# LayerNorm's 1/sqrt moved to GpSimd, and work of the softmax half moved to other steps, in a four-layer hybrid block

## The chip, the core and the metric

The kernel runs on one core of one Trainium2 chip. The metric is the device time of one execution in microseconds, lower is better. The names of the engines are those of the profile: PE is TensorE (PEld its weight loads), DVE is VectorE, ACT is ScalarE, POOL is GpSimd, SP is SyncE, which here issues most of the DMAs.

## The reference

The input x has 8 sequences of 1024 tokens with 256 features. Four layers follow each other, each on the LayerNorm of the running x and each added to it:

```python
def _layernorm(x, axis=-1, eps=1e-05):
    m = jnp.mean(x, axis=axis, keepdims=True)
    v = jnp.var(x, axis=axis, keepdims=True)
    return (x - m) / jnp.sqrt(v + eps)

x = x + linear_attention(_layernorm(x))     # 16 heads of 16, q and k through softplus, causal
x = x + ffn(_layernorm(x))                  # gated scan
x = x + softmax_attention(_layernorm(x))    # 16 heads of 16, ALiBi bias, causal
x = x + ffn(_layernorm(x))

def step(c, xt):                            # the scan of ffn, over the 8 sequences
    ft = jax.nn.sigmoid(xt @ wf.T + c @ uf.T + bf)
    it = jax.nn.sigmoid(xt @ wi.T + c @ ui.T + bi)
    gt = jnp.tanh(xt @ wc.T + c @ uc.T + bc)
    return ft * c + it * gt, None
h = jnp.tanh(jnp.einsum('tbi,oi->tbo', x, wo) + c_final @ uo.T + bo)
```

## The kernel before, in words

**Two halves.** The first half (phase 1) is linear attention and the first ffn, the second (phase 2, the softmax half) is softmax attention and the second ffn. One sequence (1024 tokens, 8 tiles of 128) is a batch. Each half is a loop over stages b = -2 to 8, and each stage has 144 steps k = 0 to 143. In stage b the attention of batch b runs, and work of the neighbours is laid between its steps: LN1 (the LayerNorm ahead of the attention) of batch b+2, q, k and v of batch b+1, and of batch b-1 the output projection, LN2 (the LayerNorm ahead of the ffn) and the gates of the scan. Each engine has its own program, written out by hand in this order; a step is not a barrier, and engines wait for each other by semaphores alone.

**A step of the softmax half.** PE computes a block of turned scores for ACT's exp (L1092, two banks in turn) and, 48 steps ahead, a block of scores whose row maxima DVE takes (`max_unit`, L1443, two banks in turn). After each fourth step PE multiplies the exps by the values (L767). So a step needs PE, DVE and ACT, and none can be more than about two steps ahead. Between them PE gets "fill": pieces of the projections and gates, in steps 4 to 10 (q, k), 16 to 22 (output), 24 to 38 (v), 40 to 54 (q, k), 60 to 66 (x times Wo) and 68 to 137 (gates).

**What the change touches, by step of a softmax stage:**

- LN2 of batch b-1: DVE takes statistics (`bn_stats`, L1510) in steps 26 to 33, aggregates 8 tiles (`bn_aggr`, L1283) and gets 1/sqrt by 12 small dependent instructions, `newton` (L1286 to L1298), in steps 34 to 40; each waits for the one before through a semaphore. POOL then subtracts and multiplies (L1744) and makes the low bf16 part (L1765), and PE turns both parts at steps 56 and 58 (L545).
- LN1 of batch b+2: statistics in steps 62 to 69 (L1525), aggregation and `newton` in steps 70 to 76, then the same on POOL. PE turns the high part at step 0 and the low part at step 2 of the next stage; ACT and DVE each copy one bank of each part out of PSUM a step later (L1085, L1383).
- The gates: ACT writes tanhs (L1165), and for each of four groups DVE makes three operations of 128x512 in fp32 (L1270, L1272, L1275), in steps 91 to 93, 104 to 106, 127 to 129 and 140 to 142. At step 143 ACT rounds the new state to bf16 (L1025, one instruction of 2048 columns), and POOL subtracts to get the low part (L1680).
- POOL's queue, in order, in the part that matters: LN1's 8 + 4 instructions, `out_low` (L1699), `split_max` (L1735, L1739), four additions of a bias row to the residual (L1829). `split_max` at steps 95 and later feeds `turn_max`, a transpose that PE has at step 99 (L781) and waits for by the semaphore mx_parts; DVE's `combine` at step 95 (L1450) comes ahead of it.

In phase 1 the same `newton` runs on DVE in steps 34 to 40 and 70 to 76; LN2 is normalised by DVE itself there. Where batches begin or end (`by_vector`) DVE normalises too.

Of the kernel before, what the change touches and what calls it, by code (L numbers as in the profile page):

```python
# [5 lines left out]
F32 = mybir.dt.float32  # L6
BF16 = mybir.dt.bfloat16
I32 = mybir.dt.int32
# [4 lines left out]
P = 128  # L13
# [40 lines left out]
LEAD = GROUP + 12  # L54
HALF_ROWS = 64
# [77 lines left out]
def mixer_kernel(nc, x, weights, cols, rows, key_rows, masks, out):  # L133
    with ExitStack() as ctx:
# [22 lines left out]
        for phase in (1, 2):  # L157
            for name in ("xa_full", "stat1_", "stat2_", "ln_norm", "ln_low", "pk_raw", "v_ready", "o_taken", "o_low",
                         "x2_in", "x3_done", "x3_out"):
                sem[f"{name}{phase}"] = ctx.enter_context(nc.semaphore(f"{name}{phase}"))  # L160
# [37 lines left out]
        NY = sb("ln_newton", [P, NT], F32)  # L198
# [326 lines left out]
        def _(pe):  # L525
# [480 lines left out]
        def _(act):  # L1006
# [118 lines left out]
            def fill_softmax(b, k):  # L1125
                nb, pb, fb = b + 1, b - 1, b + 2
                if batch_in(nb):
                    if k in (1, 3):
                        turned_in(XT1, k // 2)
# [3 lines left out]
                if batch_in(nb) and k in (31, 39):  # L1133
                    values_in(nb, 2 * (31, 39).index(k))
                if batch_in(fb) and k in (5, 9, 33, 37) and (fb or k > 9):
                    tanh_h(fb, (5, 9, 33, 37).index(k))
                if batch_in(pb):
# [10 lines left out]
                    if k == BATCH - 1 and b < B:  # L1148
                        state_high()
# [93 lines left out]
        def _(dve):  # L1243
# [4 lines left out]

            def gates(phase, group):
# [13 lines left out]
            def gate_op(group, n):  # L1263
# [7 lines left out]
                elif n == 1:  # L1271
                    step(dve.scalar_tensor_tensor(out=TG[:, 1, :], in0=TG[:, 1, :], scalar=1.0, in1=TG[:, 2, :],  # L1272
                                                  op0=ALU.add, op1=ALU.mult))
                else:
                    dve.scalar_tensor_tensor(out=cs, in0=first, scalar=0.5, in1=TG[:, 1, :],  # L1275
                                             op0=ALU.mult, op1=ALU.add).then_inc(sem["gate_used"], 1)

            def newton(which, n):

                rs = RS[:, which, :]  # L1280
                if n == 0:
                    for t in range(NT):
                        i = dve.bn_aggr(MV[:, which, t, :], ST[:, t, :])  # L1283
                    step(i)
                elif n == 1:
                    step(dve.tensor_scalar(VE[:, :], MV[:, which, :, 1], LN_EPS, None, ALU.add))  # L1286
                elif n == 2:
                    step(dve.tensor_scalar(rs.bitcast(I32), VE[:, :].bitcast(I32), 1, None, ALU.logical_shift_right))
                elif n == 3:
                    step(dve.tensor_scalar(rs.bitcast(I32), rs.bitcast(I32), -1.0, float(0x5F3759DF),  # L1290
                                           ALU.mult, ALU.add))
                elif n % 3 == 1:
                    step(dve.tensor_tensor(NY[:, :], rs, rs, ALU.mult))
                elif n % 3 == 2:
                    step(dve.scalar_tensor_tensor(out=NY[:, :], in0=NY[:, :], scalar=-0.5, in1=VE[:, :],
                                                  op0=ALU.mult, op1=ALU.mult))
                else:
                    i = dve.scalar_tensor_tensor(out=rs, in0=NY[:, :], scalar=1.5, in1=rs, op0=ALU.add, op1=ALU.mult)  # L1298
                    step(i)

            NEWTON = 13
# [18 lines left out]
            for n in range(2):  # L1320
                dve.memset(V[n].rearrange("p n (h v) -> p (n h) v", v=HV)[:, :, HD:HD + 1], 1.0)
                dve.memset(OB[n][:, :], 0.0)
            dve.memset(QKP[1][0:3 * H, 0, :], 1.0)
# [160 lines left out]
            def take_banks(b, k):  # L1484
                nb, pb = b + 1, b - 1
                if batch_in(nb):
                    if k in (1, 3):
                        turned_in(XT1, k // 2)
# [397 lines left out]
```

## Time and profile before

| | us |
|---|---|
| Device time, median of 3 runs | 2546.62 (2545.64 to 2549.15) |
| Profiled execution, span from first to last instruction | 2551.4 |
| PE busy | 2128.6 (83%) |
| DVE busy | 1689.3 (66%) |
| ACT busy | 1264.4 (50%) |
| POOL busy | 782.0 (31%) |
| Mean granted clock of PE, share of full | 0.932 |

The profile gives one time for the profiled execution, its span; it is 4.8 us above the median of the timed runs. The chain of waits (the work that ended last, followed back from the last instruction) is 63% PE, 22% DVE, 7% ACT and 4% issue. The first half takes roughly 1090 us, the softmax half the rest, of which some 160 us per full stage.

### The profile page before, as it was taken

To read this page: it belongs to the slowest core of one execution; us is meant where nothing else is said; L and a number is where in the kernel's file an instruction comes from. 1 tells how busy PE (TensorE), PEld (TensorE's weight loads), DVE (VectorE), ACT (ScalarE), POOL (GpSimd) and SP (SyncE) were. 2 spreads that over 40 slices of the span, in tenths; PEclk is the share of its full clock that TensorE was granted. 3 is DMA by queue.
4 is the path that set the end of the run, shared out by engine and by line. 5 is a ranking of instruction groups with operands and counts; after the bars stand their busy time and mean duration, and the time that the engine had idled before them with its cause. 6 is when DMAs were issued, how large, how long until landed. Compare 5 with 4: busy or idle time off the path is not lost.

```text
span 2551.4 us, 58447 instructions
## 1 busy us (share of the span) xinstructions
PE 2128.6 (83%) x24737; PEld 1221.0 (48%) x24838; DVE 1689.3 (66%) x3766; ACT 1264.4 (50%) x2041; POOL 782.0 (31%) x658
## 2 busy tenths in 40 slices
PE   3558988888797886748889999999999999998963
PEld 1346565655565564424345444454444544444432
DVE  5546474656656454348878788788787888777327
ACT  2414334343424211213676667766677666766713
POOL 2132323414143011144424335243362432412110
PEclk8789989999999988877999999999999999999977
DMA  3201010101011011134414233142331322213063
GB/s 97 66 18 43 26 51 18 62 24 51 18 35 35 18 51 47 37 110 113 117 44 121 72 84 118 41 120 76 85 117 35 117 59 76 76 35 124 12 231 132
DMA packets 131541, 179.28 MB, mean 70 GB/s; under 512 B 9121, under 2 KB 95137, under 8 KB 131281
## 3 DMA queue, kind: packets, MB, share of 16 engines
q1 hardware_dynamic: 129104, 175.02, 22.6%
q8 instruction: 196, 3.21, 0.5%
q10 hardware_dynamic: 2176, 0.52, 0.1%
q14 instruction: 65, 0.52, 0.1%
HBM read 97.40 MB, written 77.59 MB: 69 GB/s over the span
## 4 chain that ended last, share of the span: by engine, by line
PE 63%; DVE 22%; ACT 7%; issue 4%; POOL 2%; DMA 1%; SPq 0%; DVEq 0%; POOLq 0%; ACTq 0%
PE general L893 11%; PE general L579 10%; PE out_of_heads L767 9%; DVE maxima L1443 8%; PE scores L722 6%; PE general L565 4%; PE general L904 4%; PE general L545 3%; PE turned_scores L736 3%; PE out_of_heads L653 3%; PE out_of_heads L663 2%; PE scores L611 2%; PE general L553 2%; PE out_of_heads L787 1%; PE scores L671 1%
## 5 line engine op out<-in xcount | busy, mean ns | idle before, releaser
L1443 DVE TENSOR_REDUCE maxima<-scores 128x1 f32<-128x512 f32 (+3 forms) x1536 | 795.3, 552 | 228.9 <-PE scores L698 117.8
L1092 ACT ACTIVATE probs_turned<-turned_scores 128x512 f32<-128x512 f32 x1152 | 679.6, 601 | 354.7 <-PE turned_scores L698 181.4
L722 PE MATMUL scores<-k_stacks,q_stacks 59*128 59x512 bf16 (+3 forms) x1536 | 444.4, 335 | 59.2 <-DVE maxima L1443 51.6
L736 PE MATMUL turned_scores<-q_stacks,k_stacks 61*128 61x512 bf16 (+3 forms) x1536 | 436.1, 329 | 9.4 <-ACT probs_turned L1092 9.4
L722 PEld LDWEIGHTS scores<-k_stacks,q_stacks 59*128 59x128 bf16 x1536 | 124.1, 94 | 285.8 <-DVE maxima L1443 218.1
L1765 POOL TENSOR_TENSOR ln_low<-ln 128x512 bf16<-128x512 f32 x128 | 138.4, 1088 | 286.6 <-DVE ln L1425 262.6
L1744 POOL TENSOR_SCALAR ln<-x_for_attention,ln_mean_var,ln_rstd 128x256 f32<-128x256 f32 x104 | 127.9, 1239 | 187.9 <-DVEq L1532 96.6
L1680 POOL TENSOR_TENSOR state_low<-state_doubled,state_high 128x2048 bf16<-128x2048 f32 x14 | 57.0, 4068 | 363.0 <-ACT state_high L1025 363.0
L1019 ACT ACTIVATE gate_tanhs<-general,feature_vectors 128x512 f32<-128x512 f32 x96 | 66.0, 687 | 204.4 <-PE general L579 200.2
L1408 DVE TENSOR_SCALAR reciprocals<-scores 128x16 f32<-128x16 f32 x64 | 11.1, 173 | 224.4 <-PE scores L671 224.3
L767 PE MATMUL out_of_heads<-probs_turned,values 128*17 128x512 f32 (+3 forms) x1536 | 154.6, 498 | 0.0
L767 PE MATMUL out_of_heads<-probs_turned,values_odd_and_heads_out 128*17 128x512 f32 (+3 forms) x1536 | 153.0, 494 | 1.3 <-ACT probs_turned L1092 1.3
L1060 ACT COPY values_odd_and_heads_out<-out_of_heads 128x512 f32<-128x512 f32 x64 | 37.4, 585 | 233.6 <-PE out_of_heads L663 231.9
L736 PEld LDWEIGHTS turned_scores<-q_stacks,k_stacks 61*128 61x128 bf16 x1536 | 125.5, 94 | 52.0 <-ACT probs_turned L1092 18.6
L893 PE MATMUL general<-ln_turned_high,w_high 64*128 64x512 bf16 (+1 forms) x596 | 123.2, 379 | 26.7 <-ACT values L1154 11.4
L698 PE MATMUL scores<-mask_scores,identity_halves_swapped 64*128 64x128 bf16 (+1 forms) x640 | 133.9, 209 | 0.0
L698 PE MATMUL scores<-mask_scores,identity 64*128 64x128 bf16 (+1 forms) x640 | 133.8, 209 | 0.0
L698 PE MATMUL turned_scores<-mask_turned,identity 64*128 64x128 bf16 (+1 forms) x640 | 131.9, 206 | 0.0
L698 PE MATMUL turned_scores<-mask_turned,identity_halves_swapped 64*128 64x128 bf16 (+1 forms) x640 | 131.8, 206 | 0.0
L893 PE MATMUL general<-ln_turned_low,w_high 64*128 64x512 bf16 (+1 forms) x599 | 124.2, 378 | 0.1
L893 PE MATMUL general<-ln_turned_high,w_low 64*128 64x512 bf16 (+1 forms) x600 | 123.4, 377 | 0.0
L565 PE MATMUL general<-w_high,ln_turned_high 128*128 128x256 bf16 x384 | 107.0, 279 | 16.2 <-DVE ln_turned_low L1383 10.0
(252 smaller groups left out, 5347.8 us busy)
## 6 DMA issues: line engine op xcount, KB each, us to landing
x_after_attention<-x_residual SPq DMA_DIRECT2D x16, 1024.0 KB, 5.3
x_times_wo<-x_wo_out SPq DMA_DIRECT2D x64, 256.0 KB, 2.1
q_stacks<-q_stack SPq DMA_DIRECT2D x64, 256.0 KB, 4.7
k_stacks<-k_stack SPq DMA_DIRECT2D x64, 256.0 KB, 4.9
x_for_attention<-in_x SPq DMA_DIRECT2D x8, 1024.0 KB, 5.5
x_residual<-in_x SPq DMA_DIRECT2D x8, 1024.0 KB, 5.4
x_for_attention<-x_after_attention SPq DMA_DIRECT2D x8, 1024.0 KB, 5.5
ffn_h<-x_times_wo SPq DMA_DIRECT2D x32, 256.0 KB, 6.1
```

The source lines that it names most:

```text
L565: mm = pe.matmul(bank[:, n * D:(n + 1) * D], src[xp][:, k, at], W[wp][:, m, k, :], start=(i == 0), stop=(i == len(todo) - 1))
L579: mm = pe.matmul(bank[:, :], W[wp][:, m, k, e * P:(e + 1) * P], src[xp][:, k, c * CH:(c + 1) * CH], start=(n == 0), stop=(n == len(todo) - 1))
L698: return pe.matmul(columns[:, first:last + 1:step, :], eye, m, start=False, stop=(n == 1))
L722: mx = pe.matmul(bank_s[:, first * P:(first + tiles) * P], QS[at_s:at_s + QROWS, r, i * P:(i + 1) * P], KS[at_s:at_s + QROWS, r, k0 * P:(k ...
L736: ex = pe.matmul(bank_t[:, first * P:(first + tiles) * P], KS[at_t:at_t + KROWS, r, j * P:(j + 1) * P], QS[at_t:at_t + KROWS, r, i0 * P:(i ...
L767: mm = pe.matmul(OB[half][32 * g:32 * g + HV, at:at + tiles * P], values[:, j, HV * h:HV * (h + 1)], PR[:, (HEADS * unit + g) % SLOTS, fir ...
L893: return pe.matmul(bank[:, :], W[wp][rows_, m, k, e * P:(e + 1) * P], src[xp][rows_, k, c * CH:(c + 1) * CH], start=start, stop=stop)
L904: return pe.matmul(bank[:, tile * D:(tile + 1) * D], src[xp][rows_, k, t0:t0 + P], W[wp][rows_, m, k, :], start=start, stop=stop)
L1092: nc.scalar.activation(PR[:, s % SLOTS, :], TB[s % 2][:, :], ACT.Exp).then_inc(sem["ex_taken"], 1)
L1443: r = dve.tensor_reduce(MP[:, gg % 2, g, at:at + 1], max_bank[m][:, first * P:(first + tiles) * P], AX.X, ALU.max)
L1744: i = pool.tensor_scalar(XN[:, t, :], src[:, t, :], MV[:, which, t, 0:1], RS[:, which, t:t + 1], ALU.subtract, ALU.mult)
L1765: pool.tensor_tensor(pair(XL, c), pair(XN, c), top(pair(XN, c)), ALU.subtract).then_inc(sem[f"ln_low{phase}"], 1)
```

## The change

The table of steps is now at the head of the file, and the step of each operation is looked up in it. In words:

- `newton` is gone from DVE. DVE's `aggregate` does the 8 `bn_aggr` and signals POOL; `layer_norm` on POOL adds eps and raises to the power -0.5 (two instructions on 128x8), and then signals rstd. Where DVE normalises, it waits for that signal. This holds in both halves.
- Softmax half: LN2's statistics are in steps 25 to 37 with the aggregation at 38; LN1's are spread over steps 63 to 82 with the aggregation at 83.
- A group's three gate operations are 4 steps apart and not in neighbouring steps; the last one of the last group is in step 5 of the next stage. Stage 8, which has no attention, keeps them together.
- ACT's rounding of the state is in two halves of 1024 columns, at steps 19 and 23 of the next stage, and POOL's `state_low` follows after `sum_h`.
- PE turns the high part of LN1 at step 140, for batch b+2, and the low part at step 0.
- POOL's wait for the constants' DMAs is no longer at its start but ahead of the first write to the buffer that those DMAs read.

```diff
+LN2_AT = (25, 26, 27, 29, 33, 34, 35, 37)
+LN1_AT = (63, 66, 69, 71, 74, 75, 78, 82)
+GATE_AT = (((91, 95, 99), (103, 107, 111), (127, 131, 135), (139, 143)),
+           ((91, 92, 93), (104, 105, 106), (127, 128, 129), (140, 141, 142)))
+GATE_REST = 5
+HIGH_AT = (19, 23)
+TURN_AT = (140, 0)
...
             def turns(b, k):
-                if batch_in(b + 1) and k in (0, 2):
-                    if k == 0:
-                        pe.wait_ge(sem["ln_low2"], 4 * norms_to(2, "ln1", b + 1))
-                    turn_both(XN, XL, k // 2)
+                if batch_in(b + 2) and k == TURN_AT[0]:
+                    pe.wait_ge(sem["ln_norm2"], 4 * norms_to(2, "ln1", b + 2))
+                    turn_both(XN, XL, 0)
+                if batch_in(b + 1) and k == TURN_AT[1]:
+                    pe.wait_ge(sem["ln_low2"], 4 * norms_to(2, "ln1", b + 1))
+                    turn_both(XN, XL, 1)
...
-                    if k == BATCH - 1 and b < B:
-                        state_high()
+                if batch_in(pb - 1) and k in HIGH_AT:
+                    half = HIGH_AT.index(k)
+                    if half == 0:
+                        act.wait_ge(sem["gate_used"], w.next("gate_used"))
+                    i = nc.scalar.copy(CP[0][:, half, :], CS[:, half, :])
+                    if half:
+                        i.then_inc(sem["state_high"], 1)
...
+            def aggregate(phase, which, taken):
 
-            NEWTON = 13
+                dve.wait_ge(sem["dve_step"], w.at(taken))
+                for t in range(NT):
+                    i = dve.bn_aggr(MV[:, which, t, :], ST[:, t, :])
+                i.then_inc(sem[f"stat{which + 1}_{phase}"], 1)
...
+                    for group, places in enumerate(GATE_AT[b == B]):
+                        if k in places:
+                            gate_op(group, places.index(k))
+                if batch_in(pb - 1) and k == GATE_REST:
+                    gate_op(3, 2)
...
             pool.wait_ge(sem["const_ready"], w.next("const_ready"))
-            pool.wait_ge(sem["const_stored"], w.next("const_stored", 128))
...
             def layer_norm(phase, which, src, b):
                 done = 4 * (norms_to(phase, f"ln{which}", b) - 1)
+                pool.wait_ge(sem[f"stat{which}_{phase}"], b + 1)
+                pool.tensor_scalar(VE[:, :], MV[:, which - 1, :, 1], LN_EPS, None, ALU.add
+                                   ).then_inc(sem["pool_step"], 1)
+                pool.wait_ge(sem["pool_step"], w.next("pool_step"))
+                pool.tensor_tensor(RS[:, which - 1, :], VE[:, :], minus_half[:, :], ALU.pow
+                                   ).then_inc(sem[f"rstd{which}_{phase}"], 1)
...
-                if batch_in(pb - 1):
-                    state_low(2, pb - 1)
                 if batch_in(pb):
                     out_low(pb, 1)
...
+                if batch_in(pb - 1):
+                    state_low(2, pb - 1)
+                if batch_in(fb):
                     for c in (2, 3):
                         add_h(fb, c)
```

**DVE, steps 34 to 40 of a softmax stage (end of LN2).** Each line of `maxima` is one or more steps of `max_unit`. Before:

```order
L1283 BN_AGGR ln_mean_var<-ln_stats 128x2 x8
L1286 TENSOR_SCALAR ln_var_eps<-ln_mean_var 128x8
L1443 TENSOR_REDUCE maxima<-scores 128x1 x2
L1288 TENSOR_SCALAR ln_rstd<-ln_var_eps 128x8
L1290 TENSOR_SCALAR ln_rstd<-ln_rstd 128x8
L1443 TENSOR_REDUCE maxima<-scores 128x1 x2
L1293 TENSOR_TENSOR ln_newton<-ln_rstd 128x8
L1295 SCALAR_TENSOR_TENSOR ln_newton<-ln_newton,ln_var_eps 128x8
L1443 TENSOR_REDUCE maxima<-scores 128x1 x2
L1298 SCALAR_TENSOR_TENSOR ln_rstd<-ln_newton,ln_rstd 128x8
```

The same engine at the same place in the changed kernel:

```order
L1516 BN_STATS ln_stats<-x_residual 128x6
L1446 TENSOR_REDUCE maxima<-scores 128x1 x2
L1516 BN_STATS ln_stats<-x_residual 128x6
L1446 TENSOR_REDUCE maxima<-scores 128x1 x4
L1516 BN_STATS ln_stats<-x_residual 128x6
L1446 TENSOR_REDUCE maxima<-scores 128x1 x2
L1302 BN_AGGR ln_mean_var<-ln_stats 128x2 x8
L1470 COPY values_odd_and_heads_out<-general 128x32x16
```

The small dependent instructions between the maxima are gone; the last statistics and the aggregation stand where they were.

**ACT, from the last gate tanh of a stage to the first steps of the next.** Before, with the rounding of the state between the exps and both copies of LN1's turned parts after it:

```order
L1165 ACTIVATE gate_tanhs<-general,feature_vectors 128x512
L1092 ACTIVATE probs_turned<-turned_scores 128x512 x4
L1025 CAST state_high<-state_doubled 128x2048
L1092 ACTIVATE probs_turned<-turned_scores 128x512 x2
L1085 COPY ln_turned_high<-general 128x1024
L1092 ACTIVATE probs_turned<-turned_scores 128x512 x2
L1085 COPY ln_turned_low<-general 128x1024
```

And in the changed kernel:

```order
L1181 ACTIVATE gate_tanhs<-general,feature_vectors 128x512
L1101 ACTIVATE probs_turned<-turned_scores 128x512 x2
L1094 COPY ln_turned_high<-general 128x1024
L1101 ACTIVATE probs_turned<-turned_scores 128x512 x4
L1094 COPY ln_turned_low<-general 128x1024
L1101 ACTIVATE probs_turned<-turned_scores 128x512 x4
```

The high part's copy has moved to step 141, the low part's to step 1, and the rounding is gone from here.

**POOL, from LN1 to the bias additions.** Before, from the last third of LN1, which DVE signalled at the end of step 76:

```order
L1744 TENSOR_SCALAR ln<-x_for_attention,ln_mean_var,ln_rstd 128x256 x2
L1765 TENSOR_TENSOR ln_low<-ln 128x512 x2
L1699 TENSOR_TENSOR attention_out_low<-attention_out 128x8x128
L1735 CAST maxima_parts<-maxima 128x16 x2
L1739 TENSOR_TENSOR maxima_parts<-maxima,maxima_parts 128x16 x2
L1829 TENSOR_TENSOR x_residual<-x_residual,row_vectors 128x512 x4
```

In the changed kernel the queue is the same behind LN1, which now begins with two more instructions and is signalled at the end of step 83:

```order
L1759 TENSOR_SCALAR ln_var_eps<-ln_mean_var 128x8
L1762 TENSOR_TENSOR ln_rstd<-ln_var_eps,minus_half 128x8
L1752 TENSOR_SCALAR ln<-x_for_attention,ln_mean_var,ln_rstd 128x256 x4
L1779 TENSOR_TENSOR ln_low<-ln 128x512
L1752 TENSOR_SCALAR ln<-x_for_attention,ln_mean_var,ln_rstd 128x256 x2
L1779 TENSOR_TENSOR ln_low<-ln 128x512
L1752 TENSOR_SCALAR ln<-x_for_attention,ln_mean_var,ln_rstd 128x256 x2
L1779 TENSOR_TENSOR ln_low<-ln 128x512 x2
L1705 TENSOR_TENSOR attention_out_low<-attention_out 128x8x128
L1743 CAST maxima_parts<-maxima 128x16 x2
```

`split_max` (the last row) still stands behind LN1 and `out_low`.

## Rows read from the trace of the kernel before

**Rows 1.** Windows, two whole stages: busy time of each engine, its instructions, granted clock.

```profile
1474.86:1634.01 159.15, 153.00 (x1895) 77.64 (x1894) 128.90 (x293) 111.10 (x194) 65.32 (x63) 1.00 0.31 88
1794.72:1955.42 160.70, 154.54 (x1895) 78.49 (x1894) 128.98 (x293) 111.31 (x194) 65.31 (x63) 0.99 0.31 87
```

**Rows 2.** Windows around LN2 and LN1 of stage 4, columns PE, PEld, DVE, ACT, POOL.

```profile
1827.00:1848.00 21.00, 18.85 (x269) 9.97 (x267) 20.05 (x62) 13.39 (x25) 6.27 (x9) 1.00 0.45 124
1876.00:1887.00 11.00, 10.79 (x155) 6.08 (x150) 10.31 (x44) 6.66 (x13) 0.93 (x1) 1.00 0.61 175
```

**Rows 3.** Chain of waits, LN2 of stage 4: start, duration, what.

```profile
1831.84 0.69 DVE maxima L1443
...
1839.58 0.18 DVE ln_var_eps L1286
...
1841.62 0.87 DVE ln_newton L1293
...
1847.31 0.23 PE scores L722
```

**Rows 4.** Chain of waits, the first LayerNorm of the softmax half.

```profile
1093.82 0.65 DVE ln_mean_var L1283 x8
1094.50 0.18 DVE ln_var_eps L1286
...
1097.03 4.85 DVE ln L1425 x8
```

**Rows 5.** Chain of waits, LN2 of one stage of phase 1.

```profile
578.53 0.18 DVE ln_newton L1293
...
580.73 0.18 DVE ln_rstd L1298
```

**Rows 6.** Chain of waits, the edge between stages 4 and 5.

```profile
1955.42 1.76 issue
...
1959.21 1.89 PE general L545 x16
```

**Rows 7.** Window just after that edge.

```profile
1959.00:1962.40 3.40, 3.19 (x28) 2.22 (x32) 1.91 (x6) 2.64 (x5) 2.42 (x1) 0.50 0.28 55
```

**Rows 8.** Timeline of POOL in stage 3, from LN1 to the bias additions.

```profile
1725.36 4.83 POOL L1744 TENSOR_SCALAR ln<-x_for_attention,ln_mean_var,ln_rstd 128x256 f32<-128x256 f32 x4 [16.37 <-DVEq L1532]
...
1738.98 1.89 POOL L1699 TENSOR_TENSOR attention_out_low<-attention_out 128x1024 bf16<-128x1024 f32 x1
1745.42 0.33 POOL L1735 CAST maxima_parts<-maxima 128x16 bf16<-128x16 f32 x2 [4.55 <-DVE maxima L1450]
...
1746.18 4.95 POOL L1829 TENSOR_TENSOR x_residual<-x_residual,row_vectors 128x512 f32<-128x512 f32 x4
```

**Rows 9.** Timeline of DVE there: steps 82 and 83, and two gate operations.

```profile
1730.42 1.47 DVE L1443 TENSOR_REDUCE maxima<-scores 128x1 f32<-128x512 f32 x2
...
1739.70 1.72 DVE L1270 SCALAR_TENSOR_TENSOR gate_tanhs<-gate_tanhs,state_doubled 128x512 f32<-128x512 f32 x1
...
1741.94 0.67 DVE L1272 SCALAR_TENSOR_TENSOR gate_tanhs<-gate_tanhs 128x512 f32<-128x512 f32 x1
```

**Rows 10.** Timeline of PE there, `turn_max` at step 99.

```profile
1749.24 0.24 PE L781 MATMUL scores<-identity,maxima_parts 128*64 128x128 bf16 x1
```

**Rows 11.** Timeline of DVE in stage 0, steps 82 and 83.

```profile
1262.19 1.28 DVE L1443 TENSOR_REDUCE maxima<-scores 128x1 f32<-128x512 f32 x2
```

**Rows 12.** Timeline of PE in stage 0, `turn_max` at step 99.

```profile
1278.55 0.24 PE L781 MATMUL scores<-identity,maxima_parts 128*64 128x128 bf16 x1
```

**Rows 13.** Groups by line, POOL: a small cast, and its costliest elementwise form.

```profile
L1715 POOL TENSOR_SCALAR probs_turned<-qk_block,mask_even_odd 128x1024 f32<-128x1024 f32 x16 | 46.3, 2903 | 33.7 <-DVE qk_block L1421 33.7
...
L1735 POOL CAST maxima_parts<-maxima 128x16 bf16<-128x16 f32 x64 | 10.5, 196 | 357.6 <-DVE maxima L1450 357.6
```

**Rows 14.** Chain of waits, stage 7: LN2 on POOL, and the rounding of the state.

```profile
2320.91 4.83 POOL ln L1744 x4
...
2422.35 1.60 issue
```

More of the change, by code:

```diff
@@ L1271, in gate_op @@
                 elif n == 1:
-                    step(dve.scalar_tensor_tensor(out=TG[:, 1, :], in0=TG[:, 1, :], scalar=1.0, in1=TG[:, 2, :],
-                                                  op0=ALU.add, op1=ALU.mult))
+                    dve.scalar_tensor_tensor(out=TG[:, 1, :], in0=TG[:, 1, :], scalar=1.0, in1=TG[:, 2, :],
+                                             op0=ALU.add, op1=ALU.mult).then_inc(sem["dve_step"], 1)
+                    taken["gate"] = w.later("dve_step")
                 else:
+                    dve.wait_ge(sem["dve_step"], w.at(taken["gate"]))
                     dve.scalar_tensor_tensor(out=cs, in0=first, scalar=0.5, in1=TG[:, 1, :],
                                              op0=ALU.mult, op1=ALU.add).then_inc(sem["gate_used"], 1)
[L1278 to L1299, printed above, removed]
-            NEWTON = 13
+            def aggregate(phase, which, taken):
[3 more added lines that the diff above has]
+                i.then_inc(sem[f"stat{which + 1}_{phase}"], 1)
             def last_state_low(phase, half):
@@ L1564, in fill @@
                         if k == 33:
-                            step(i)
-                    if 34 <= k < 41:
-                        for n in range(2 * (k - 34), min(2 * (k - 34) + 2, NEWTON)):
-                            newton(1, n)
+                            i.then_inc(sem["dve_step"], 1)
+                            taken[1] = w.later("dve_step")
+                    if k == 34:
+                        aggregate(1, 1, taken[1])
                     if k in (45, 47, 48, 50):
                         if k == 45:
+                            dve.wait_ge(sem["rstd2_1"], pb + 1)
                             dve.wait_ge(sem["xt_dve"], turned_before(1, "ln2", pb))
@@ L1583, in fill @@
                         if at == 69:
[L1584 to L1589 removed]
+                            i.then_inc(sem["dve_step"], 1)
+                            taken[0] = w.later("dve_step")
+                    if at == 70:
+                        aggregate(1, 0, taken[0])
                     if by_vector(1, 1, fb) and at == 77:
+                        dve.wait_ge(sem["rstd1_1"], fb + 1)
                         if turned_before(1, "ln1", fb):
@@ L1711, in split_q @@
                 pool.wait_ge(sem["phi_done"], 4 * nb + 2 * e + 1)
+                if nb == 1 and e == 0:
+                    pool.wait_ge(sem["const_stored"], w.next("const_stored", 128))
                 if nb >= 2:
```

77 lines of the change are left out of this document (37 added, 40 removed).

## The prediction

> **What bounds the kernel now.** I read the busy shares first: PE is near its limit and DVE has a third of its time free, so most work taken from DVE should be worth nothing. The windows of whole stages say the same of the softmax half: in a stage of 159 or 161 us PE is busy for 153 to 155 us and DVE for 129 us [rows 1]. So what counts is where a stage is not PE's. Two windows answer that. Around LN2 (steps 25 to 43) DVE is busy for 20.05 of 21.00 us and PE for only 18.85; around LN1 (steps 67 to 78) DVE has 10.31 of 11.00 us, but PE has 10.79, so both are full there [rows 2]. The chain of waits, read last, confirms it: from 1831.84 to 1847.31 us, 15.5 us without a break, every piece is DVE's, maxima with statistics and `newton` instructions between them, and then it goes back to PE [rows 3]. At the edge of two stages the chain is ACT's: 1.76 us of "issue" behind the start of the state's rounding, then exps and the copy of the turned LN1, until PE's second turning begins at 1959.21, 3.8 us after 1955.42 [rows 6]. Right behind it PE's granted clock is 0.50, which is 1.2 GHz, for 3.4 us [rows 7]. The stage that began without such a fall took 159.15 us and the one with it 160.70, with the same 1895 matmuls [rows 1]: the fall costs 1.5 us. Four edges of the same kind show such a fall.
>
> **LN2 in the softmax half.** One `newton` costs, from the end of the aggregation to the first normalisation with nothing between, 1097.03 - 1094.50 = 2.5 us: 12 instructions of 0.18 us and their waits [rows 4]. In a stage its pieces stand between maxima at nearly the same price; one of them even takes 0.87 us [rows 3]. The aggregation (0.65 us) stays. In the 15.5 us of DVE's own chain 2.5 us go. PE is not idle beneath: it has 2.15 us free in the 21 us window [rows 2], and its modelled ends stretch where it waits, so the gain can be as low as 1.0; above, with the locked 0.87 us instruction and the earlier statistics, it is 2.8. I take 2.5, because the chain is DVE's throughout. Six stages (1 to 6): 15.0 us. In stage 7, which has no q, k, v of a next batch, PE is not late; there the chain goes on through POOL's LN2 from 2320.91 [rows 14]. The signal now comes two steps earlier and without `newton`: 2.5 + 2 x 0.76 (a step of maxima) - 0.6 (new work on POOL, below) = 3.4 us.
>
> **LN1 in the softmax half.** The same 2.5 us go from DVE, but PE is full there [rows 2]; at the end of that stretch some PE time was lost. I take 0.3 us for six stages, 1.8 us (between 0 and 1.9 each).
>
> **The new instructions on POOL.** No row of before shows a power on POOL. The nearest is a small one, 0.20 us for a cast of 16 columns; the costliest elementwise instruction takes 2.9 us, though for 1024 columns [rows 13]. The new ones have 8 columns, so I take the small row: 0.2 for eps, 0.3 for the power, 0.15 for two semaphores, 0.65 us in all; I keep 0.4 and 3 as ends.
>
> **Serial LayerNorms.** Five times DVE makes a LayerNorm with nothing beside it: two at the start, the last of phase 1, the first of phase 2 [rows 4] and the last of all. Each gives 2.5 - 0.65 = 1.9 us: 9.5 us. The turning of the first of phase 2 no longer waits for the first low part: 1.1 us more. Sum 10.6 us. POOL's wait for the constants, moved away from its start, must go with it, since POOL's signal now stands ahead of the first normalisation.
>
> **LN2 in phase 1.** The chain of one stage holds two pieces of `newton`, three instructions from 578.53 and two up to 580.91 [rows 5], 1.0 us together; seven stages show the same: 7.0 us (3 to 9). There DVE normalises from step 45 on, ten steps after the signal, so POOL's 0.65 us is hidden. LN1 in phase 1 is on no chain: nothing.
>
> **The edge.** The rounding leaves ACT's queue between the exps (1.76 us of the chain), and one of two turnings leaves the first three steps, with its copy, for step 140, where PE has no fill, but where DVE is busy with gate operations; DVE gets the 0.69 us copy there and gives two of its gate operations away. Of the 3.8 us [rows 6] the two exps stay, and some of the turning's 1 us comes back at step 140. I take 2.0 us, with 1.0 and 3.2 as bounds, for the six edges from 1-2 to 6-7: 12.0 us. The four falls of the clock go with the idle time that comes ahead of them, 4 x 1.5 = 6.0 us. At the last edge the rounding's 1.6 us goes [rows 14]. Sum 19.6 us. In its new place the rounding lies in steps 19 and 23, each half about 1 us, where PE's fill is long and ACT has slack; I charge 1.0 us for all stages. `state_low` (4 us) moves with it on POOL, ahead of add_h, which waits for a tanh of step 33 anyway: nothing.
>
> **What gets worse: POOL at step 99.** LN1 is now signalled at the end of step 83 and not 76. Before, POOL began LN1 at 1725.36, was through with it and with `out_low` at 1740.87, and then sat idle for 4.55 us until `combine` let `split_max` go [rows 8]. This idle time is used up. In before, from the end of step 83 on DVE (1730.42 + 1.47 = 1731.89) [rows 9] to `turn_max` on PE (1749.24) [rows 10] there are 17.35 us. In the changed kernel these must hold: 0.3 for the statistics of step 82, 0.65 aggregation, 0.65 the new instructions, 13.62 LN1 (1725.36 to 1738.98), 1.89 `out_low`, 0.76 `split_max` [rows 8], and 0.6 for two gate operations that now meet LN1. That is 18.5 us. So PE's `turn_max` waits for POOL, DVE and ACT run out two steps behind it, and the stage loses 1.1 us at this place, in stages 1 to 5: -5.5 us. In stage 0, which has no gates and little fill, only 1278.55 - 1263.47 = 15.1 us are there [rows 11, 12] against 17.9: -2.8 us. Stages 6 and 7 have no LN1, and spreading the gate operations gives 0.8 us in each, since the first took 1.72 us against 0.67 for its neighbour [rows 9]: +1.6. Sum -6.7 us (-20 to 0).
>
> The gate operation of 1.72 us began at 1739.70, while POOL's `out_low` ran until 1740.87; it ended 0.55 us after that, so it waited for POOL's instruction to end [rows 8, 9]. The Trainium skill (SBUF — State Buffer, Who interferes with whom) has this as a rule: a DVE instruction with two SBUF inputs and a GpSimd instruction that reads SBUF exclude each other for a whole instruction, and the first to start wins. The trace agrees here. By the rule all of the operations at steps 91, 95, 99 and 103 would meet a POOL that has no gap, each waiting up to 1.2 us or holding POOL for 0.67 us, and the stage would lose about 1 us more than I charge, 5 us in all; the forecast would then be 2502 us, inside its own range.
>
> **Sum.** 15.0 + 3.4 + 1.8 + 10.6 + 7.0 + 19.6 - 1.0 - 6.7 = 49.7 us. The profiled execution's own time, its span, is 2551.4 us, so 2501.7; it is 4.8 us above the median of the timed runs, 2546.62, and I take the same distance off: 2497 us, 2.0% faster.
>
> **Rivals.**
>
> 1. PE is the bound everywhere. For it: PE's busy time in a stage leaves only 6 us [rows 1]. Against it: the chain around LN2 has no PE in it [rows 3]. Then LN2 gives 1.0 and not 2.5, an edge 1.0 and not 2.0: 9 + 6 = 15 us less, 2512 us.
> 2. The power is slow on POOL, about 2 us. It counts wherever POOL is waited for: at step 99 of six stages and in five serial LayerNorms, 11 x 1.7 = 19 us: 2516 us. Nothing in the trace speaks for or against it but the small instructions [rows 13].
> 3. The stall moves instead of going: PE's wait at step 99 takes the clock down as the one at the edge did [rows 7], six times 1.5 us, and the four falls at the edges stay: 9 + 6 us, 2512 us. For it: the wait would be as long as PE's pause at an edge. Against it: each wait at step 99 is a single one.
> 4. Slower than before: the same queue of POOL at step 99 decides. It needs 50 us in all, that is a power of more than 0.3 + 50/11 = 4.8 us on POOL in these 11 places; at 6.3 us, twice the costliest instruction of [rows 13], it would be 2497 + 66 = 2563 us.
>
> **How the numbers follow.** Forecast 0.57 (2485 to 2508), rival 1 0.16, rival 2 0.13, rival 3 0.10, rival 4 0.04. All but the last and the far end of the second (0.02) are faster by over 0.2%, about what a measurement can tell from no change here: faster 0.94, within it 0.02, slower 0.04. The range goes from 2478 (an edge at 3.2, LN2 at 2.8 and nothing lost at step 99 would be 2481) to 2522, past rivals 1 to 3.
>
> **What would show it.** Right: the chain around LN2 has no small DVE instructions and changes to PE early; a full stage of the softmax half takes about 155 us; no 0.50 clock at the edges; PE's L781 of step 99 waits for POOL's `maxima_parts` for 1 to 2 us in stages 0 to 5, and POOL has no idle time between LN1, `out_low` and `split_max`; the power takes 0.2 to 0.4 us. Wrong: a power of microseconds; a chain that goes through POOL in the middle of the stage for several us; stages 1 to 5 no shorter than 158 us; a new wait at step 140, where PE's turning needs ACT's last gate tanh, or at steps 19 and 23, where exps wait behind the rounding.

## The result, and the profile after

| | before | changed |
|---|---|---|
| Device time, median of 4 runs, us | 2547.89 (2545.64 to 2551.01) | 2531.91 (2528.0 to 2538.07) |
| Ratio, 95% interval | | 0.9933 (0.9914 to 0.9952) |
| Span of the profiled execution, us | 2551.4 | 2536.3 |
| DVE busy, us | 1689.3 | 1644.2 |
| POOL busy, us | 782.0 | 852.0 |

The change makes the kernel 0.7% faster, not the 2.0% of the forecast, and 2531.91 us lies 10 us outside the range. The sign was right and the size was missed by 35 us. The profiled execution is the longest of the four, 6 us above their median. Sections 1 and 4 of the profile's page show what shifted: DVE's share of the chain fell from 22% to 16%, and POOL's rose from 2% to 7%.

```profile
PE 2113.1 (83%) x24737; PEld 1221.7 (48%) x24838; DVE 1644.2 (65%) x3383; ACT 1260.8 (50%) x2048; POOL 852.0 (34%) x722
...
PE 65%; DVE 16%; ACT 8%; POOL 7%; issue 4%; DMA 1%; SPq 0%; DVEq 0%; POOLq 0%; ACTq 0%
```

Two whole stages of the changed kernel, stages 1 and 3, beside the stages 2 and 4 of [rows 1] (columns PE, PEld, DVE, ACT, POOL, granted clock, DMA share, GB/s). They are hardly shorter than the 159.15 and 160.70 us of before, with DVE's busy time unchanged to 1 us although `newton` has left it, and PE's lower by up to 2.8 us. 3 us of what DVE is busy with is a blocked instruction, as shown below.

```profile
1314.49:1473.13 158.64, 151.77 (x1896) 78.61 (x1894) 127.99 (x268) 108.96 (x193) 66.91 (x66) 0.99 0.31 88
1633.06:1791.92 158.86, 151.77 (x1896) 78.71 (x1894) 128.38 (x269) 110.57 (x195) 70.91 (x67) 0.99 0.31 88
```

**Where in a stage.** ACT's exp (L1092 before, L1101 after) starts once a step, 1152 times in all. The difference in the time between two such starts, after less before, places every microsecond. Each figure is that of the profiled executions, in us:

| steps | stage 0 | each of stages 1 to 5 | stage 6 | stage 7 | all stages |
|---|---|---|---|---|---|
| 24 to 47 (LN2) | 0.0 | -2.97 | -2.18 | -2.88 | -19.9 |
| 48 to 59 | 0.0 | 0.05 to 0.27 | 0.05 | 2.30 | 2.9 |
| 60 to 95 (LN1) | -3.8 | -1.04 | 0.0 | 0.0 | -9.1 |
| 96 to 119 (step 99) | 8.0 | 5.35 to 6.65 | 0.0 | 0.3 | 38.2 |
| 120 to 143 and 0 to 23 (edge) | 0.6 | -1.9, with a fall of the clock gone -3.5 | -2.5 | -1.8 | -17.8 |

The sum is -5.7 us. Another -8.2 us stand ahead of the first exp (phase 1 and the serial LayerNorms) and -1.3 us behind the last: -15.1 us before rounding, the difference of the two spans. So everywhere but at one step 53 us were won, where the forecast had 49.7 + 8.3 = 58 us without its charge for step 99, and 38 us of them went at that step.

**LN2.** The chain of waits of the changed kernel in stage 4, at the place of [rows 3]. DVE's own piece (its end is shown) has no small `newton` instruction in it any more, and from 1824.86 us the chain is PE's. Where DVE's chain had 15.5 us without a break, its longest piece is now 6.0 us, from 1818.88 to 1824.86.

```profile
1822.96 0.34 DVE ln_stats L1516
1823.29 0.59 DVE maxima L1446
1823.88 0.33 DVE ln_stats L1516
1824.22 0.60 DVE maxima L1446
1824.86 0.39 PE scores L729
1825.32 0.44 PE general L911 x8
```

**Step 99.** The chain of waits in stage 3. From the end of the aggregation to PE's turning of the parts it is POOL's for 19.9 us.

```profile
1724.04 0.56 DVE ln_mean_var L1302 x8
...
1724.68 0.25 POOL ln_var_eps L1759
...
1725.01 1.68 POOL ln_rstd L1762
...
1726.78 4.83 POOL ln L1752 x4
...
1741.42 1.85 POOL attention_out_low L1705
1743.27 0.75 POOL maxima_parts L1743 x2
...
1744.09 0.40 POOL maxima_parts L1747 x2
...
1744.54 0.31 PE scores L788
```

The timeline of POOL there, answering to [rows 8]. The power takes 1.67 us where 0.3 was assumed. Of the eight instructions of LN1 (L1752), the first four take 4.83 us as before, and the two later pairs 2.86 and 2.95 us. A pair with nothing beside it takes 2.42 us (a row of the first experiment's kernel further down).

```profile
1725.01 1.67 POOL L1762 TENSOR_TENSOR ln_rstd<-ln_var_eps,minus_half 128x8 f32<-128x8 f32 x1
...
1732.61 2.86 POOL L1752 TENSOR_SCALAR ln<-x_for_attention,ln_mean_var,ln_rstd 128x256 f32<-128x256 f32 x2
...
1736.47 2.95 POOL L1752 TENSOR_SCALAR ln<-x_for_attention,ln_mean_var,ln_rstd 128x256 f32<-128x256 f32 x2
1739.39 2.03 POOL L1779 TENSOR_TENSOR ln_low<-ln 128x512 bf16<-128x512 f32 x2
1741.38 1.89 POOL L1705 TENSOR_TENSOR attention_out_low<-attention_out 128x1024 bf16<-128x1024 f32 x1
1743.22 0.79 POOL L1743 CAST maxima_parts<-maxima 128x16 bf16<-128x16 f32 x2
```

DVE and PE on the same timeline. The gate operation of step 99 takes 3.54 us and not 0.68: it begins while POOL runs `ln_low`, and ends 0.6 us after `out_low` does. PE stands still for 3.92 us ahead of L788, and a matmul of 512 columns then takes 0.60 us where it took 0.38.

```profile
1740.28 3.54 DVE L1295 SCALAR_TENSOR_TENSOR state_doubled<-gate_tanhs 128x512 f32<-128x512 f32 x1
```

```profile
1739.26 0.38 PE L729 MATMUL scores<-k_stacks,q_stacks 59*128 59x512 bf16 x1
...
1744.54 0.31 PE L788 MATMUL scores<-identity,maxima_parts 128*64 128x128 bf16 x1 [3.92 <-POOL maxima_parts L1747]
1744.78 0.60 PE L729 MATMUL scores<-k_stacks,q_stacks 59*128 59x512 bf16 x1
```

Windows show the clock there (columns as above). PE has 0.02 us of work in 3.60 us, and in the 3.40 us behind it the granted clock is 0.50, that is 1.2 and not 2.4 GHz.

```profile
1740.60:1744.20 3.60, 0.02 (x3) 0.00 (x0) 3.22 (x1) 0.00 (x0) 3.52 (x5) 1.00 0.94 299
1744.20:1747.60 3.40, 3.06 (x23) 1.31 (x25) 0.94 (x2) 1.07 (x3) 3.40 (x5) 0.50 0.47 149
```

In the softmax steps before, 20.5 us ran at half clock, 13.7 of them right behind four edges; in the changed kernel it is 44.4 us, of which 34 us stand behind step 99 in stages 0 to 5. None stands right behind an edge, but the fall that before had in step 1 of stage 7 is not gone: it stands in step 10 and costs about 1.6 us there.

### The profile page after: what moved, and what is told of

Read it like the earlier page. It is cut to its first block, busy times and chain, and to the rows that moved or that the text cites. A ratio compares the mean times of both kernels' runs of the same rounds, so it can differ in the third digit from the quotient of the medians.

```text
span 2536.3 us, 58000 instructions
## 1 busy us (share of the span) xinstructions
PE 2113.1 (83%) x24737; PEld 1221.7 (48%) x24838; DVE 1644.2 (65%) x3383; ACT 1260.8 (50%) x2048; POOL 852.0 (34%) x722
## 4 chain that ended last, share of the span: by engine, by line
PE 65%; DVE 16%; ACT 8%; POOL 7%; issue 4%; DMA 1%; SPq 0%; DVEq 0%; POOLq 0%; ACTq 0%
PE general L900 11%; PE general L586 10%; PE out_of_heads L774 9%; PE scores L729 6%; PE general L911 4%; DVE maxima L1446 4%; PE general L572 4%; PE turned_scores L743 3%; POOL ln L1752 3%; PE general L552 3%; PE out_of_heads L660 3%; PE scores L618 2%; PE out_of_heads L670 2%; PE general L560 2%; PE scores L705 1%
## 5 line engine op out<-in xcount | busy, mean ns | idle before, releaser
L1101 ACT ACTIVATE probs_turned<-turned_scores 128x512 f32<-128x512 f32 x1152 | 678.7, 601 | 333.0 <-PE turned_scores L705 174.7
L729 PE MATMUL scores<-k_stacks,q_stacks 59*128 59x512 bf16 (+3 forms) x1536 | 447.3, 337 | 49.7 <-DVE maxima L1446 46.2
L1069 ACT COPY values_odd_and_heads_out<-out_of_heads 128x512 f32<-128x512 f32 x64 | 37.4, 585 | 222.3 <-PE out_of_heads L670 220.6
L1759 POOL TENSOR_SCALAR ln_var_eps<-ln_mean_var 128x8 f32<-128x8 f32 x32 | 7.9, 248 | 389.4 <-DVE ln_mean_var L1302 389.4
L1752 POOL TENSOR_SCALAR ln<-x_for_attention,ln_mean_var,ln_rstd 128x256 f32<-128x256 f32 x104 | 132.4, 1283 | 1.4
L1393 DVE TENSOR_TENSOR probs_turned<-scores,mask_keep 128x512 f32<-128x512 f32 x128 | 84.1, 685 | 67.7 <-PE turned_scores L618 67.5
L1743 POOL CAST maxima_parts<-maxima 128x16 bf16<-128x16 f32 x64 | 16.0, 280 | 324.4 <-DVE maxima L1453 324.4
```

What stands on the lines that cost most here:

```text
L729: mx = pe.matmul(bank_s[:, first * P:(first + tiles) * P], QS[at_s:at_s + QROWS, r, i * P:(i + 1) * P], KS[at_s:at_s + QROWS, r, k0 * P:(k ...
L1101: nc.scalar.activation(PR[:, s % SLOTS, :], TB[s % 2][:, :], ACT.Exp).then_inc(sem["ex_taken"], 1)
L1752: i = pool.tensor_scalar(XN[:, t, :], src[:, t, :], MV[:, which, t, 0:1], RS[:, which, t:t + 1], ALU.subtract, ALU.mult)
```

## The experiments

Times are medians of 4 runs with 95% intervals against the kernel before on the same chip. "Gap" is PE's idle time ahead of L788 at step 99, "loss" the difference to before in steps 96 to 107, both for stages 1 to 5. The medians of the kernel before in these comparisons lie between 2547.89 and 2549.8 us, so times of different rows can be compared to within about 2 us.

| | us | ratio | gap | loss |
|---|---|---|---|---|
| changed kernel | 2531.91 | 0.9933 (0.9914 to 0.9952) | 3.92 | 5.4 to 6.7 |
| e1 LN1's statistics early | 2489.7 | 0.9768 (0.9753 to 0.9782) | none | 0 |
| e2 split_max inside LN1 | 2496.89 | 0.9792 (0.9778 to 0.9807) | none | 0.6 |
| e3 product for power | 2502.99 | 0.982 (0.9804 to 0.9837) | 1.63 | 1.95 |
| e4 power twice (one run) | 2538.09 | | 4.90 | 6.8 to 7.1 |
| e5 only the power moved | 2509.57 | 0.9843 (0.9829 to 0.9858) | none | 0 |
| e6 = e1, rounding back | 2512.33 | 0.9853 (0.9837 to 0.987) | none | 0 |
| e7 = e1, turning back | 2489.43 | 0.9764 (0.9749 to 0.9778) | none | 0 |
| e8 first gate group together | 2518.71 | 0.9879 (0.9864 to 0.9894) | 2.59 | 2.9 to 4.1 |
| e9 power and rounding only | 2488.15 | 0.9759 (0.9743 to 0.9776) | none | 0 |

**e1: LN1's statistics back in steps 62 to 69.** The theory is that POOL's queue at step 99 costs what is missing.

```diff
-LN1_AT = (63, 66, 69, 71, 74, 75, 78, 82)
+LN1_AT = (62, 63, 64, 65, 66, 67, 68, 69)
```

> The changed kernel with LN1's statistics back in steps 62 to 69 and its aggregation in step 70; all else as changed. Theory A (the loss is the wait of PE at step 99 for split_max, which stands behind LN1 in GpSimd's queue, because LN1 is signalled at step 83): in the changed kernel steps 96 to 107 are 5.4 to 6.7 us longer in stages 1 to 5 and 8.0 us in stage 0; all of that goes, and up to 1 us per stage comes back around LN1 on VectorE: 2532 - 30 - 8 + 7 = about 2501 us, PE's gap ahead of L788 zero, no half clock in mid-stage. Rival B (VectorE and GpSimd meet at the shared port because the gate operations are spread, whatever LN1 does): steps 96 to 107 keep 3 us or more each, 2515 to 2532 us.

It took 2489.7 us, 42 less than the changed kernel, by this one line. No gap and no half clock are left in the softmax steps. In the traces 37.9 of the 45.7 us between the two kernels lie in steps 96 to 119. The timeline of POOL in stage 3: LN1's last pair takes 2.42 us, `out_low` ends at 1707.05, and POOL then has 7.21 us to spare before `combine` lets `split_max` go, more than the 4.55 us of before.

```profile
1700.77 2.42 POOL L1752 TENSOR_SCALAR ln<-x_for_attention,ln_mean_var,ln_rstd 128x256 f32<-128x256 f32 x2
...
1705.15 1.90 POOL L1705 TENSOR_TENSOR attention_out_low<-attention_out 128x1024 bf16<-128x1024 f32 x1
1714.26 0.72 POOL L1743 CAST maxima_parts<-maxima 128x16 bf16<-128x16 f32 x2 [7.21 <-DVE maxima L1453]
```

**e2: split_max ahead of the last quarter of LN1.** The signal stays late, and only the order on POOL changes.

```diff
+                    if inside and c == 2:
+                        inside()
...
-                    layer_norm(2, 1, XA, fb)
+                    layer_norm(2, 1, XA, fb, (lambda: split_max(GROUPS * b + 3)) if early else None)
```

> The changed kernel with one thing moved in GpSimd's queue: in stages 0 to 5 split_max of step 95 stands inside LN1, behind its third quarter, ahead of the last pieces and of out_low; LN1 is signalled at step 83 as in the changed kernel. Theory A: the wait at step 99 goes although LN1 is as late as before, 2532 - 30 - 7 = about 2496 us; GpSimd may now wait for VectorE's combine for up to 1 us, which costs nothing. Rival B (port): gate operations still meet LN1 and out_low, and with VectorE blocked for up to 3.5 us at step 99 its maxima come late: PE loses 2 us or more per stage, 2508 to 2520 us.

The gaps are gone here too, at 2496.89 us. In stage 3 the CAST of `split_max` now starts 6 us before `out_low` and not behind it. So it is the place of `split_max` in POOL's queue that PE waits for, and LN1 itself, late as it is, costs only 0.6 us a stage.

```profile
1714.14 0.72 POOL L1743 CAST maxima_parts<-maxima 128x16 bf16<-128x16 f32 x2
...
1720.16 1.89 POOL L1705 TENSOR_TENSOR attention_out_low<-attention_out 128x1024 bf16<-128x1024 f32 x1
```

**e3: the power replaced by a product**, so the 1/sqrt is left out of the output, and nothing else is.

```diff
-                pool.tensor_tensor(RS[:, which - 1, :], VE[:, :], minus_half[:, :], ALU.pow
+                pool.tensor_tensor(RS[:, which - 1, :], VE[:, :], minus_half[:, :], ALU.mult
```

> The changed kernel with GpSimd's power replaced by a product of the same shape, so that the output lacks the 1/sqrt; everything else, waits included, is as changed. It prices the power, 1.67 us in the profile of the changed kernel, against about 0.2 us. Theory A: 1.45 us less in each of six waits at step 99 (8.7 us, more where the clock then does not fall), in five LayerNorms with nothing beside them (7 us) and in stage 7 (1.5 us): about 2514 us, the gap ahead of L788 2.4 us instead of 3.9. Rival C (the power is hidden, and the gap is made by the locked instructions): under 3 us in all, 2529 us or more.

The product takes 0.20 us, 1.47 less than the power, so the small row that I had taken [rows 13] holds for a product and not for a power. The gap shrinks by 2.3 us and not by 1.47 alone, since LN1 also takes 13.65 us and not 14.60: the gate operations meet POOL's queue elsewhere (the one at step 99 takes only 1.25 us). No fall of the clock follows the gap in stages 1 to 5. The time falls by 28.9 us to 2502.99. By the count of 11 places it would be 16 us: the power's price is nearly doubled by what it sets off.

```profile
1710.51 0.20 POOL L1762 TENSOR_TENSOR ln_rstd<-ln_var_eps,minus_half 128x8 f32<-128x8 f32 x1
```

```profile
1727.61 0.24 PE L788 MATMUL scores<-identity,maxima_parts 128*64 128x128 bf16 x1 [1.63 <-POOL maxima_parts L1747]
```

**e4: a second power on POOL**, whose result nobody reads, in the LN1 of the softmax half.

```diff
+                if phase == 2 and which == 1:
+                    pool.tensor_tensor(spare[:, :], VE[:, :], minus_half[:, :], ALU.pow)
```

> The changed kernel with a second, unused power ahead of the first, in LN1 of the softmax half alone. Theory A: every us that GpSimd is later is a us of PE at step 99: the gap ahead of L788 grows from 3.9 to 5.6 us in stages 1 to 5, the whole by 6 x 1.7 = 10 us, about 2542 us. Rival C: the gap stays at 3.9 to 4.5 us.

The gap is 4.90 us, 1.0 more, and not the full 1.67 us. POOL's queue shows why: it is shifted, so the gate operations fall elsewhere in it; LN1 takes 14.30 us and `split_max` 0.76, against 14.60 and 1.22, and the pair of L1753 shown below is back at 2.43 us. One run gave 2538.09 us, the same as the profiled execution of the changed kernel (2538.07), so the price of the longer gap isn't shown by the total; the loss in steps 96 to 107 is 6.8 to 7.1 us against 5.4 to 6.7.

```profile
1728.08 1.67 POOL spare_power L1764
1729.74 1.62 POOL ln_rstd L1765
...
1737.56 2.43 POOL ln L1753 x2
```

**e5: the kernel before with nothing but 1/sqrt on POOL**, the aggregation signalling at steps 34 and 70; every other part of the change is left out but the move of the wait for the constants, which the power needs.

> The kernel before, with only 1/sqrt moved to POOL in both halves; statistics, gate operations, rounding and turning stand where they were, and the aggregation now signals at step 70 (LN1) and step 34 (LN2), six steps earlier than newton's end did. Theory (DVE's chain around LN2 is what the power relieves, and step 99 is lost only where LN1 is signalled late): LN2 gives 2.5 to 2.9 us in each of stages 1 to 6, stage 7 gives 3, phase 1 and the serial LayerNorms together 8 to 10, step 99 has no gap ahead of the turn and steps 96 to 107 are within 0.5 us of before, the edges give nothing: 2549 - (16 + 3 + 9) = 2521 us, 2515 to 2527. Rival (the gain at steps 36 to 47 comes from the statistics' new steps): that range changes by under 1 us a stage, and the time is about 2535. Rival (two more POOL instructions are enough for a gap at step 99, whatever the signal): a gap over 1 us there, 2530 or more.

2509.57 us, 11 less than I expected and 22 less than the whole change. Steps 36 to 47 gain 2.82 us a stage with the statistics where they were, so that gain is the power's. Steps 72 to 95 gain 1.17 us in stages 1 to 5 and 3.0 us in stage 0. The edge between two stages gains nothing, but two of the four falls of the clock there are gone (1.5 us each). A full stage of it, windows:

```profile
1769.51:1924.67 155.16, 151.40 (x1892) 78.36 (x1892) 123.99 (x268) 110.77 (x194) 69.25 (x68) 1.00 0.31 90
```

**e6: e1 with the rounding of the state whole at step 143 again**, and the last gate group at 140 to 142.

```diff
-                if batch_in(pb - 1) and k in HIGH_AT:
-                    ...
+                if batch_in(pb) and k == BATCH - 1 and b < B:
+                    state_high()
```

> LN1's statistics in steps 62 to 69 as in e1_ln1_early, and the state's rounding whole at step 143 again, with the last group of gate operations at 140 to 142. Theory (of the edge's gain the larger part is ACT's rounding, the 1.76 us of issue in before's chain): six edges lose 1.3 to 1.8 us each against e1_ln1_early, 2498 to 2500 us. Rival (the turning of LN1 is what counts at the edge): under 4 us lost, 2492 to 2494. Rival (the clock's fall comes back with the idle time too): half clock stretches reappear right behind the edges, and the loss is above 12 us.

It lost 22.6 us against e1, as much as the last of the three cases wanted, though only a fifth of it is the clock's: 2.18 us in steps 132 to 143 of each stage, 1.62 in the last, and 4.5 us in steps 0 to 11, where four falls of the clock are back (13.7 us at half clock against none). The chain of waits at the edge between stages 3 and 4 shows the 1.63 us behind it, as [rows 6] did:

```profile
1771.22 0.17 ACT state_high L1034
1771.39 1.63 issue
1773.03 1.07 ACT probs_turned L1101 x2
```

**e7: e1 with both turnings of LN1 at steps 0 and 2 again.**

```diff
-                if batch_in(b + 2) and k == TURN_AT[0]:
-                    ...
+                if batch_in(b + 1) and k in (0, 2):
+                    ...
```

> LN1's statistics in steps 62 to 69 as in e1_ln1_early, and both turnings of LN1 at steps 0 and 2 again. Theory (the rounding is the larger part of the edge): the turning costs 0.5 to 1.2 us an edge, 2493 to 2497 us, in steps 0 to 11, with steps 132 to 143 giving a little of it back. Rival (the turning counts most): 8 us or more lost, 2498 or above.

2489.43 us, the same as e1. Steps 132 to 143 get 0.60 us a stage back, and steps 0 to 11 lose 0.24. Moving the turning had no worth; I had expected 0.5 to 1.2 us an edge.

**e8: the changed kernel with the first gate group back in steps 91 to 93.**

```diff
-GATE_AT = (((91, 95, 99), (103, 107, 111), (127, 131, 135), (139, 143)),
+GATE_AT = (((91, 92, 93), (103, 107, 111), (127, 131, 135), (139, 143)),
```

> The changed kernel with the first group of gate operations back at steps 91, 92 and 93, so that none stands at step 99, where DVE's gate operation waited 3.54 us for POOL. Theory (the gap at step 99 is POOL's queue of LN1, out_low and split_max; the blocked DVE operation lies beside it): the gap stays at 3 to 4 us, stages 1 to 5 change by under 1 us each, 2528 to 2532 us. Rival (the spread gate operations and the shared SBUF port make the gap): the gap falls below 2 us and the time to 2515 or less.

I had expected no more than 1 us a stage. The gap fell by 1.33 us to 2.59, the loss by 2 to 3.7 us, and the time by 13 us to 2518.71. So the blocked gate operation isn't beside the path: when it ends its wait it holds POOL's CAST (0.79 us for two in the changed kernel, 0.33 here), and LN1 takes 14.07 us (1720.97 to 1735.04) and not 14.60. These two are 1.0 of the 1.33 us; the other 0.33 us is that PE comes to step 99 that much later, since steps 84 to 95 give 0.33 us less. In stage 0 the gap stays at 5.30 us. In four of stages 1 to 5 no fall of the clock follows the shorter gap; the stage with a fall lost 4.08 us, those without 2.91. So one fall costs 1.2 us at this place. The rest of the gap stays, so both theories have a part. POOL's timeline:

```profile
1735.04 1.89 POOL L1705 TENSOR_TENSOR attention_out_low<-attention_out 128x1024 bf16<-128x1024 f32 x1
1736.88 0.33 POOL L1743 CAST maxima_parts<-maxima 128x16 bf16<-128x16 f32 x2
```

```profile
1737.73 0.24 PE L788 MATMUL scores<-identity,maxima_parts 128*64 128x128 bf16 x1 [2.60 <-POOL maxima_parts L1747]
```

**e9: two parts alone, the power on POOL and the rounding at steps 19 and 23.** Statistics, gate operations and turning stand as before.

```diff
-LN2_AT = (25, 26, 27, 29, 33, 34, 35, 37)
+LN2_AT = (26, 27, 28, 29, 30, 31, 32, 33)
-GATE_AT = (((91, 95, 99), (103, 107, 111), (127, 131, 135), (139, 143)),
+GATE_AT = (((91, 92, 93), (104, 105, 106), (127, 128, 129), (140, 141, 142)),
...
-                if batch_in(pb - 1) and k == GATE_REST:
-                    gate_op(3, 2)
```

(against e7's kernel)

> Only two parts of the change: 1/sqrt on POOL, and ACT's rounding of the state at steps 19 and 23; statistics, gate operations and turning stand as in the kernel before. Theory (these two make the whole gain, the spread statistics and gate operations are worth nothing): against e5_power_alone six edges gain 2.3 us and the last one 1.6, and what clock falls are left at edges go, so 2488 to 2493 us, the same as e7_turning_back (2489.43) within 0.2%. Rival (part of the edge's gain is the last group's third gate operation, which left step 142): steps 132 to 143 gain under 1.5 us an edge and the time is 2495 or more. Rival (spreading LN2's statistics helps): steps 24 to 47 lose over 0.5 us a stage against e7_turning_back, 3 us or more in all.

2488.15 us, 2.4% under before and 1.7% under the changed kernel. It has the lowest median, and e1 and e7 are the same within their spread. Against e7, steps 24 to 47 differ by 0.01 us a stage: spreading LN2's statistics brings 0.43 us in steps 24 to 35 and costs 0.43 in 36 to 47. All of the changed kernel's gain is in these two parts, and the other moves bring nothing or cost. A stage of it:

```profile
1759.80:1912.64 152.84, 150.73 (x1896) 78.36 (x1894) 123.25 (x269) 110.54 (x194) 69.13 (x67) 1.00 0.32 91
```

## Why the prediction was wrong, step by step

- **What bounds the kernel: right.** DVE around LN2, ACT's rounding at the edge, PE elsewhere. Rival 1 is out: LN2 and the edge gave their full size.
- **LN2 in the softmax half: right.** 15.0 us forecast for stages 1 to 6; 17.0 measured (five times 2.97 and 2.18), and e5 shows that it is `newton`'s. In stage 7 the 3.4 us came to 0.6, since 2.30 of 2.88 us went again in steps 48 to 59, behind POOL's LN2; a fall of the clock stands there in the changed kernel, and e7, without one, loses 0.96.
- **LN1: sized too low.** 1.8 us forecast, 9.1 measured in steps 60 to 95, of which 3.8 in stage 0. I had read "PE is full" from 10.79 of 11.00 us [rows 2], a window that ends at step 78; the gain lies partly behind it, in steps 84 to 95, which I had not looked at.
- **The edge: right in sum, wrong in its split.** 2.0 us an edge and 1.5 for a fall; measured 1.9 and 1.5 in stages 1 to 5. Three of the four falls went; the fourth only moved, from step 1 to step 10 of stage 7. But the rounding alone is worth 2.2 us (e9), and the turning was to give part of it and costs 0.36 net (e7). The 1.0 us charged for steps 19 and 23 was not there: steps 12 to 23 changed by 0.0 in all full stages.
- **Phase 1 and the serial LayerNorms: too high.** Ahead of the first exp 15.7 us were forecast (7.0 and 8.7) and 8.2 measured; the experiments with the same first half (without e3 and e4, which change the number or kind of powers in it) have 8.7 to 13.7. A serial LayerNorm now waits 2.12 us for POOL (row below) where `newton` took 2.53 with its waits [rows 4], so each of the five gives 0.4 us and not 1.9; this is the power's price again. And LN2 in phase 1 gives next to nothing in stages 1 to 6. From stage 1 to stage 7, by the first start in each of ACT's copy of `out_of_heads` (L1069), the lead over before grew by 0.5 us in the changed kernel, 0.4 in e5 and 2.5 in e9, against 6 that I had counted. Between the first and the last of these copies in stage 7 it grew by another 3.5 us in the changed kernel and by 1.0 in e5, which stays unexplained. In the stage of [rows 5] the pieces of `newton` left the chain, but behind ACT's `ffn_h` the next piece stood nearly as late. A piece in the chain of one stage is not worth its length in every stage.

```profile
1089.80 4.84 DVE L1428 TENSOR_SCALAR ln<-x_for_attention,ln_mean_var,ln_rstd 128x256 f32<-128x256 f32 x8 [2.12 <-POOL ln_rstd L1762]
```

- **Step 99: the step that failed.** I charged 1.1 us in each of stages 1 to 5 and 2.8 in stage 0, 8.3 us in sum. Steps 96 to 119 lost 38.2 us in the trace, and taking the cause away gave 42 us on the clock (e1). The place and the mechanism were named rightly, and three sizes were not:
  1. The power: 1.67 us, not 0.3; the two new instructions and their semaphores take 2.10 us (1724.68 to 1726.78) and not 0.65. I had taken the value near the cheapest row although an end of 3 us was open, and put 0.13 on the rival of a slow power. With the power as a product the loss is 1.95 us.
  2. POOL's work beside DVE's gate operations: LN1 14.60 us (1726.78 to 1741.38), not 13.62, and 1.22 for `split_max` (1743.22 to 1744.44), not 0.76. Two gate operations were counted with 0.6 us; the further 1 us a stage of all four of them stood in the prediction as a case of its own and not in the sum. e8 gives 13 us for the first group alone. I also counted 17.35 us of time until the turning, by the trace of before; PE reaches it 0.7 us sooner now, since steps 84 to 95 are shorter.
  3. A gap isn't worth its length. 3.92 us of gap became 5.4 to 6.7 us of stage. Where the clock held (e3, e8), the stage lost 0.32 us more than the gap. So of the changed kernel's loss 1.1 to 2.4 us is the clock's: it is at 0.50 for 3.4 us behind the gap where least was lost, and for 6.8 us where most was. My rival 3 had this, with a chance of 0.10; against it I had only that each wait is a single one; that wait was 1.1 us in the forecast and 3.92 on the chip.
- **How the cases were combined.** The sum took each new cost at its small end, and rivals 2 and 3 were priced one by one at 2516 and 2512 us. The slow power makes the gap that takes the clock down, so they come together: 49.7 - 19 - 15 = 15.7 us, near the 15.1 measured (partly by luck, as 6 of the 15 were falls at edges, of which three went). The range reached only past each alone. (In rival 4, twice 2.9 us is 5.8 and not 6.3 us; nothing hangs on it.)
- **Gate operations.** The 1.6 us for spreading them in stages 6 and 7 were not there (0.0 in steps 84 to 107).

The Trainium skill (SBUF — State Buffer, Who interferes with whom) says that a DVE instruction with two SBUF inputs and a GpSimd instruction that reads SBUF contend, and that the one blocked waits for a whole instruction of the other. The trace agrees and goes further: the gate operation that began at 1740.28 waited out the last 0.1 us of one `ln_low`, the whole of the next (1.03 us) and all of `out_low` (1.89 us), two whole instructions in a row, and took 3.54 us.

Not settled: why four of the six edges showed a fall of the clock before, and where up to 5.5 us ahead of the first exp come from, between kernels with the same first half, and up to 5.3 us behind the last exp, between the changed kernel and e7 or e9 (their half-clock stretches lie differently there); the experiments don't separate it.

## What to carry to other kernels

Moving work from a full engine to an idle one is paid for in the idle one's queue: list what stands behind it there, and who waits for that. Here `split_max`, 1 us of work behind 19 us of LayerNorm and `out_low`, cost 38 us, and either an earlier signal (e1) or another place in the queue (e2) gave it back. Price an operation that the trace doesn't show at the dear end until it has been measured alone, and add to a long pause of PE what the clock may take behind it (here 1.1 to 2.4 us behind 3.92, nothing behind 1.63).

## What the runs showed of the hardware

- A power on POOL over 128x8 fp32 takes 1.67 us (32 instances, 1.665 to 1.672); a product of the same shape 0.20 us, an addition of a constant 0.25 us.
- A DVE operation of 0.68 us with two SBUF inputs took 3.54 us beside a POOL without a pause, in each of stages 1 to 5, and two of POOL's instructions of 1.21 us beside such operations took 1.65 to 1.75 us there.
- Behind PE gaps of 3.92 us (5.29 in stage 0) the granted clock was 0.50 for 3.4 or 6.8 us, in all of stages 0 to 5 of the changed kernel; behind gaps of 4.90 us for 6.8 us in all of stages 1 to 5 (e4); behind gaps of 2.59 us in one of five stages (e8), and behind gaps of 1.63 us in none of five (e3).
